# First maximum pass over four PSUM banks, page clears and a late load moved, side steps of a turn re-placed, gathers two groups sooner

## The reference, cut to what matters

```
h = layernorm(x) * (1 + ca) + sa
q, k, v = split(h @ qkv_w.T + qkv_b);  q, k = rope(q), rope(k)
attn = softmax(causal(q k^T / sqrt(8)));  x = x + ga * (attn v @ proj_w.T + proj_b)
h = layernorm(x) * (1 + cb) + sb
probs = sigmoid(h @ router_w.T + expert_bias); top 8 of 160, weights scaled by 2.5 / their sum
x = x + gb * (sum over the 8 experts of w_down(silu(w_gate h)) + shared expert)
```

## Time and profile before

| What | Value |
|---|---|
| median of 3 runs | 2018.66 us (2017.83 to 2021.72) |
| the profiled execution, its own time | 2040.86 us |
| its span, first to last instruction | 2038.9 us |
| mean granted TensorE clock | 0.887 |
| PE, DVE, ACT, POOL busy | 77%, 58%, 41%, 50% of the span |

### The profile page before, as it was taken

How to read it: one execution, slowest core, us unless ns; L and a number is a source line. 1 busy time by engine, 2 the same in 40 slices (tenths; PEclk the granted TensorE clock), 3 DMA queues, 4 the chain that set the end, 5 groups by cost and what they waited for, 6 DMA issues and landing times.

```text
span 2038.9 us, 35388 instructions
## 1 busy us (share of the span) xinstructions
PE 1565.4 (77%) x12102; PEld 792.8 (39%) x12102; DVE 1185.1 (58%) x2998; ACT 826.2 (41%) x1717; POOL 1021.8 (50%) x1057
## 2 busy tenths in 40 slices
PE   5558877788788778877877668966888888888875
PEld 2224433343343334333333345643444444444431
DVE  4657876687678767777766526633444444444434
ACT  1045544453445445445544434323343333343421
POOL 2001355555665556555645510056666666666663
PEclk9989888997898779778977678978999999999988
DMA  5695455554555545545542258986777777777631
GB/s 161 178 303 159 140 150 149 167 158 141 158 167 157 143 135 168 143 140 170 168 113 74 79 188 283 334 274 185 240 237 229 212 240 222 239 239 239 207 106 56
DMA packets 264986, 369.70 MB, mean 181 GB/s; under 512 B 41207, under 2 KB 141832, under 8 KB 264680
## 3 DMA queue, kind: packets, MB, share of 16 engines
q1 hardware_dynamic: 214248, 268.81, 45.5%
q0 software_dynamic: 28672, 58.78, 9.5%
q10 hardware_dynamic: 21888, 39.86, 5.2%
HBM read 219.69 MB, written 147.60 MB: 180 GB/s over the span
## 4 chain that ended last, share of the span: by engine, by line
PE 46%; DVE 20%; issue 12%; another core or an unknown queue 12%; ACT 5%; SPq 2%; DMA 2%; ACTq 1%; POOL 1%; DVEq 0%
DVE block_max L598 9%; PE bank L1715 6%; PE bank L743 5%; PE bank L1739 4%; PE bank L1578 4%; PE bank L1557 3%; PE bank L1594 3%; PE bank L569 3%; PE bank L680 2%; ACT prob L707 2%; PE bank L692 2%; PE bank L452 2%; PE bank L582 2%; PE bank L1720 1%
## 5 line engine op out<-in xcount | busy, mean ns | idle before, releaser
L1646 POOL DMA_INDIRECT vh<-results,pos_all x448 | 454.3, 1014 | 351.6 <-PE bank L1313 125.3
L818 POOL DMA_INDIRECT pages<-h,pos_s x448 | 433.2, 967 | 262.5 <-issue 103.7
L598 DVE TENSOR_REDUCE block_max<-bank 128x4 f32<-128x512 f32 x640 | 411.9, 683 | 245.7 <-PE bank L582 112.6
L707 ACT ACTIVATE prob<-bank 128x512 f32<-128x512 f32 x640 | 349.4, 598 | 465.9 <-PE bank L692 245.3
L1733 DVE TENSOR_TENSOR work<-work,bank 128x512 f32<-128x512 f32 x160 | 110.1, 688 | 358.1 <-issue 187.8
L569 PE MATMUL bank<-km,qm 64*128 64x512 bf16 (+3 forms) x1024 | 203.2, 343 | 112.2 <-DVE block_max L598 65.7
L680 PE MATMUL bank<-qe,ke 64*128 64x512 bf16 (+3 forms) x1024 | 174.9, 341 | 96.3 <-issue 57.2
L743 PE MATMUL bank<-prob,v_ext 128*32 128x512 f32 (+3 forms) x2048 | 225.7, 506 | 8.3 <-issue 5.3
L1608 ACT ACTIVATE v_ext<-bank 128x256 f32<-128x256 f32 x254 | 87.0, 387 | 199.9 <-remote 84.3
L569 PEld LDWEIGHTS bank<-km,qm 64*128 64x128 bf16 x1024 | 51.6, 97 | 276.6 <-issue 164.6
L1594 PE MATMUL bank<-prob,ke 64*128 64x128 f32 x1216 | 114.4, 309 | 52.3 <-ACT ke L1586 37.0
(11 more groups left out here) (221 smaller groups left out, 2542.4 us busy)
## 6 DMA issues: line engine op xcount, KB each, us to landing
prob<-wexp SPq DMA_DIRECT2D x448, 96.0 KB
pages<-free_rows SPq DMA_DIRECT2D x38, 1024.0 KB
prob<-pages SPq DMA_DIRECT2D x152, 256.0 KB
results<-v_ext ACTq DMA_DIRECT2D x152, 256.0 KB
qm<-q_stacks SPq DMA_DIRECT2D x64, 256.0 KB
km<-k_stacks SPq DMA_DIRECT2D x64, 256.0 KB
qe<-q_stacks SPq DMA_DIRECT2D x64, 256.0 KB
ke<-k_stacks SPq DMA_DIRECT2D x64, 256.0 KB
```

What stands on the lines that cost most here:

```text
L598: e.tensor_reduce(block_max[:, at, :], MX[g % 2][:, :].rearrange("p (k t) -> p k t", t=P), AX.X, ALU.max).then_inc(s_mxd, 1)
L707: e.activation(prob[:, slot, :], ST[g % 3][:, :], ACT.Exp, scale=SCALE).then_inc(s_exa, 1)
L818: e.indirect_dma_start(out=pages, in_=h2[:, t, :], in_offset=None, out_offset=bass.IndirectOffsetOnAxis(ap=pos_s[:, t * TOPK + k:t * TOPK ...
L1646: e.indirect_dma_start(out=y8[:, i, k, :], out_offset=None, in_=results[0:ready(n) * GRP * P, :], in_offset=bass.IndirectOffsetOnAxis(ap=p ...
```

## The change

- The first maximum pass (n = 0) uses banks 0 to 3 in turn, and a unit waits for the reduction of unit g - 4. The four projections of sequence 0 go to banks 6, 4, 5 and 3 and don't wait for DVE's reading of each other.
- The stores of q and k are split: four of the six transfers wait only for the second part (ACT, line 491), two for the third (POOL, line 495).
- Clears: of the twelve first ones, none are in turn -1, five in turn 0 and six in turn 1; the pairs come one turn later (turns 2 to 14). The load of sequences 9 to 15 moves from turn 0 to turn 2 with a semaphore of its own.
- Places: new lists for `pre` and for the two halves of the routing; the end of the maximum pass from 0.015 to 0.037 (ACT at 0.054, SP at 0.071), the first exponential load from 0.03 to 0.077, the two next maximum loads from 0.87 to 0.92 to 0.962; the page table's counts from 0.55 to 0.9 to 0.33 to 0.66 of turn 15.
- Last routing: spread over 0.9 of a merge with 34 groups instead of 0.62 of 30; both exponentials of ACT in one step; the reciprocal of line 1185 cut in four steps. The row numbers of the gathers are worked out at group 34 instead of 32.
- Gathers of tile T at group 49 + 2T instead of 51 + 2T, and its sum two groups sooner too.

```diff
-Q_RUNS = ((0, (0, 0, 0)), (3, (1, 1)), (5, (2,)))
-K_RUNS = ((0, (0, 1, 2)), (3, (0, 1)), (5, (0,)))
+Q_SOON, Q_LAST = ((0, (0, 0, 0)), (3, (1, 1))), ((5, (2,)),)
+K_SOON, K_LAST = ((3, (0, 1)), (5, (0,))), ((0, (0, 1, 2)),)
+        FIRST_MX = bank[0:4]
...
-                    e.wait_ge(s_x, (16, 32, 48, 80)[n])
+                    e.wait_ge(s_x, 16 * (n + 1))
+                if n == 9:
+                    e.wait_ge(s_x9, 16)
...
+                to_a, to_b = (MA, MA) if n > 0 else (MA, bank[4]) if w == "q" else (bank[5], bank[3])
-                    else:
+                    elif n > 0:
                         pre_d.wait(e, prev + "_b", n)
-                    pre_p.done(e.matmul(MA[:, :], col["w" + w], hT[:, :], start=True, stop=True), w + "_a")
+                    pre_p.done(e.matmul(to[:, :], col["w" + w], hT[:, :], start=True, stop=True), w + "_a")
...
+                    if runs in (Q_LAST, K_LAST):
+                        pre_g.wait(e, w + "_3", n)
+                    else:
+                        pre_a.wait(e, w + "_2", n)
...
-            steps = steps[:8] + stores[0:1] + steps[8:] + stores[1:2]
+            steps = steps[:8] + stores[0:2] + steps[8:] + stores[2:4]
...
+            banks = FIRST_MX if n == 0 else MX
+            mine = banks[g % len(banks)]
-                wait(e, s_mxd, n * 4 * UNITS + g - 1)
+                wait(e, s_mxd, n * 4 * UNITS + g + 1 - len(banks))
...
-            def sigmoid(e):
-                full_a.wait(e, "exp", m)
-                full_d.done(e.tensor_scalar(logit[:, :, :], logit[:, :, :], 1.0, 0.4, ALU.add, ALU.mult), "one")
-                full_d.wait(e, "one", m)
-                full_d.done(e.reciprocal(logit[:, :, :], logit[:, :, :]), "sig")
+            def sigmoid(e, t):
+                if t == 0:
+                    full_a.wait(e, "exp", m)
+                    full_d.done(e.tensor_scalar(logit[:, :, :], logit[:, :, :], 1.0, 0.4, ALU.add, ALU.mult), "one")
+                    full_d.wait(e, "one", m)
+                last = e.reciprocal(logit[:, t, :], logit[:, t, :])
+                if t == NT - 1:
+                    full_d.done(last, "sig")
...
-            steps.append({"dve": choose, "act": sig})
-            steps.append({"dve": weigh, "act": exps})
-            steps += [{"dve": f} for f in (sigmoid, combine_weights, part1, part2)]
+            steps.append({"dve": choose, "act": lambda e: [sig(e), exps(e)]})
+            steps.append({"dve": weigh})
+            steps += [{"dve": lambda e, t=t: sigmoid(e, t)} for t in range(NT)]
+            steps += [{"dve": f} for f in (combine_weights, part1, part2)]
...
-        PRE_AT = (0.021, 0.061, 0.15, 0.207, 0.274, 0.36, 0.422, 0.474, 0.481, 0.553, 0.611, 0.636, 0.688, 0.751)
+        PRE_AT = (0.003, 0.036, 0.154, 0.193, 0.273, 0.360, 0.438, 0.468, 0.470, 0.470, 0.563, 0.590, 0.590, 0.617, 0.633, 0.704)
...
-                streams.append((core(i), 0.0, 0.98, 0.95))
+                streams.append((core(i), 0.0, 0.978, 0.95))
-                streams.append(([{"pe": end_turn, "act": end_keep, "sp": end_store}], 0.015, 0.015))
-                streams.append((exp_loads(i, (0,)), 0.03, 0.03))
-                streams.append((exp_loads(i, (1,)), 0.28, 0.28))
-                streams.append((exp_loads(i, (2,)), 0.53, 0.53))
-                streams.append((exp_loads(i, (3,)), 0.78, 0.78))
-            if i <= 0:
-                streams.append((first_clears()[(0, 1, 5)[i + 2]:(1, 5, Z0)[i + 2]], (0.6, 0.45, 0.2)[i + 2], 0.9))
-                if i > -2:
-                    streams.append((x_loads(2, 4) if i == -1 else x_loads(4, 9) + x_loads(9, NB), 0.1, 0.6))
-            elif i < PAGED:
-                streams.append((clears(i), 0.3, 0.7))
+                streams.append(([{"pe": end_turn, "act": end_keep, "sp": end_store}], 0.037, 0.034))
+                streams.append((exp_loads(i, (0,)), 0.077, 0.077))
+                streams.append((exp_loads(i, (1,)), 0.276, 0.276))
+                streams.append((exp_loads(i, (2,)), 0.511, 0.511))
+                streams.append((exp_loads(i, (3,)), 0.798, 0.798))
+            if i <= 1:
+                streams.append((first_clears()[(0, 1, 1, 6)[i + 2]:(1, 1, 6, Z0)[i + 2]], (0.6, 0.45, 0.15, 0.15)[i + 2], 0.9))
+                if i in (-1, 0):
+                    streams.append((x_loads(2, 4) if i == -1 else x_loads(4, 9), 0.1, 0.6))
+            elif i <= PAGED:
+                streams.append((clears(i - 1), 0.3, 0.7))
+            if i == 2:
+                streams.append((x_loads(9, NB, s_x9), 0.15, 0.15))
...
-                streams.append((max_loads(i + 2, (0, 1)), 0.87, 0.92))
+                streams.append((max_loads(i + 2, (0, 1)), 0.962, 0.962))
...
-                streams.append((table(), 0.55, 0.9))
+                streams.append((table(), 0.33, 0.66))
...
-        FIRST, SPREAD = 30, 32
+        FIRST, SPREAD = 34, 32
...
-            return 51 + 2 * T
+            return 49 + 2 * T
...
-                        if k == SPREAD and name == "dve":
+                        if k == FIRST and name == "dve":
...
-            return merge((routing(NB - 1), 0.0, 0.62, 0.6), ([b_step(G) for G in range(FIRST)], 0.02, 1.0, 0.0))
+            return merge((routing(NB - 1), 0.0, 0.9, 0.6), ([b_step(G) for G in range(FIRST)], 0.02, 1.0, 0.0))
```

More of the change, by code:

```diff
@@ L231, in build @@
         MX, ST, PV, MA, MB = bank[0:2], bank[2:5], bank[5], bank[6], bank[7]
-        s_w, s_const, s_x, s_zero, s_set, s_zfill, s_rest = (
-            sem(n) for n in ("s_w", "s_const", "s_x", "s_zero", "s_set", "s_zfill", "s_rest"))
+        FIRST_MX = bank[0:4]
+        s_w, s_const, s_x, s_x9, s_zero, s_set, s_zfill, s_rest = (
+            sem(n) for n in ("s_w", "s_const", "s_x", "s_x9", "s_zero", "s_set", "s_zfill", "s_rest"))
         s_modd, s_modp, s_moda = sem("s_modd"), sem("s_modp"), sem("s_moda")
@@ L362, in mcol, with x_loads @@
             return mod[:, j, bass.ds(n, 1)]
-        def x_loads(first, last):
+        def x_loads(first, last, landed=s_x):
             return [{"sp": lambda e: e.dma_start(
                 xr[:, first * NT:last * NT, :].rearrange("p (n t) d -> p n t d", t=NT),
-                x[first:last].rearrange("n (t p) d -> p n t d", p=P)).then_inc(s_x, 16)}]
+                x[first:last].rearrange("n (t p) d -> p n t d", p=P)).then_inc(landed, 16)}]
         ZG = 4
@@ L457, in rope_a, with proj_b, rope_b @@
                         pre_d.wait(e, "q", n)
-                    pre_d.done(e.scalar_tensor_tensor(out=rot_a[:, :], in0=MA[:, :], scalar=col["b" + w], in1=cosT,
+                    pre_d.done(e.scalar_tensor_tensor(out=rot_a[:, :], in0=to[:, :], scalar=col["b" + w], in1=cosT,
                                                       op0=ALU.add, op1=ALU.mult), w + "_a")
-                def proj_b(e, w=w):
-                    pre_d.wait(e, w + "_a", n)
-                    pre_p.done(e.matmul(MA[:, :], col["w" + w + "r"], hT[:, :], start=True, stop=True), w + "_b")
-                def rope_b(e, w=w):
+                def proj_b(e, w=w, to=to_b):
+                    if n > 0:
+                        pre_d.wait(e, w + "_a", n)
+                    pre_p.done(e.matmul(to[:, :], col["w" + w + "r"], hT[:, :], start=True, stop=True), w + "_b")
+                def rope_b(e, w=w, to=to_b):
                     pre_p.wait(e, w + "_b", n)
-                    pre_d.done(e.scalar_tensor_tensor(out=rot_b[:, :], in0=MA[:, :], scalar=col["b" + w + "r"],
+                    pre_d.done(e.scalar_tensor_tensor(out=rot_b[:, :], in0=to[:, :], scalar=col["b" + w + "r"],
                                                       in1=sinT, op0=ALU.add, op1=ALU.mult), w + "_b")
@@ L496, in part3, with store @@
                                w + "_3")
-                def store(e, w=w):
-                    pre_g.wait(e, w + "_3", n)
+                def store(e, runs, w=w):
+                    if runs in (Q_LAST, K_LAST):
+                        pre_g.wait(e, w + "_3", n)
+                    else:
+                        pre_a.wait(e, w + "_2", n)
                     stacks = (qd if w == "q" else kd)[bass.ds(n, 1)].rearrange("o a r (g t) -> (o a) r g t", t=S)
-                    for first, parts in (Q_RUNS if w == "q" else K_RUNS):
+                    for first, parts in runs:
                         m = len(parts)
@@ L512, in pre @@
                 steps.append({"act": part2, "pool": part3})
-                stores.append({"sp": store})
+                soon, last = (Q_SOON, Q_LAST) if w == "q" else (K_SOON, K_LAST)
+                stores += [{"sp": lambda e, f=store, runs=runs: f(e, runs)} for runs in (soon, last)]
             def v_proj(e):
@@ L576, in hide @@
                 if m == 1:
-                    return e.matmul(MX[g % 2][:, at:at + 64], corner, eye_half[rows_, :],
+                    return e.matmul(mine[:, at:at + 64], corner, eye_half[rows_, :],
                                     start=False, stop=True, skip_group_check=True)
```

(6 more changed lines are left out.)

21 lines of the change are left out of this document (9 added, 12 removed).

## The result

The changed kernel takes 2030.97 us (median of 6 runs, 2024.6 to 2038.43), the kernel before 2020.35 on the same chip (6 runs): ratio 1.0057, interval [1.0032, 1.0082]. It is slower by 0.6%; the forecast was 2% faster. Its profiled execution took 2037.12 us (span 2035.2) against 2040.86. The profiled execution of the kernel before is 20 us over its median, that of the changed one 6 us, so the two spans hide the loss and I compare stretches.

The account below looks back on a forecast made before the run. No single engine was taken as the limit; PE was nearest, with step order deciding its lost time. Terms summed to 40.7 us off the profiled 2040.86, giving 2000.2, times 0.989: 1978 us, range 1955 to 2000.

Parts of the forecast that it names:

- the gathers' term: End of the kernel: last gathers wait for the last results whatever their number; one weighing comes off, 1.2 us won.
- Projections and first pass: Sequence 0's projections run back to back, 2.5 us off; four banks overlap PE and DVE in first maximum pass, 14 off.
- Turns 0 and 1: Moved clears and input load remove two thirds of PE's load waits, 13 us, less 4 in turn 1: net 9 off.
- my sign: Turn 0, expected if the forecast was right: no wait for a load over 4 us.
- rival 1: Turns 0 and 1: the clog only moves, 9 us given back, and the places gain nothing: 1996 us, chance 0.15.
- The end of each pass: End of each maximum pass: PE's wait at the turning of the maxima goes; 6 us off, ends 11 and 0.
- The other places: Side steps and loads at new places in the turns: a new order takes or gives a little; 3 us off.
- Tail: Routing of the last two sequences: cut reciprocal, no table load, chain spread over more groups; 5 us off, ends 8 and 0.
- Rival 2: First maximum pass is paced by its loads, 7 us won instead of 14: 1985 us, chance 0.12.
- rival 3: New places pay 1 us more in each of thirteen turns and PE's 11 us are all won: 1961 us, chance 0.16.
- rival 5: Whole change: the parts don't do what they say, or undo each other: 2018 us, chance 0.02.
- Rival 4: Slower: first exponential load, 3.2 us later in each of fourteen turns, comes after its quad is due: 2034 us, chance 0.05.

Follow-up runs that it names:

- a_burst: Changed kernel with gathers at 51 + 2T, the first 16 gathers of each sequence let go at once: 2097.66 us, 1.0364 of the kernel before.
- r_f50: Changed kernel with gathers at group 50 + 2T instead of 49 + 2T: 1980.58 us, 0.9767 of the kernel before.
- a_f51: Changed kernel with gathers back at group 51 + 2T, sums following: 1996.97 us, 0.9789 of the kernel before.
- u_clears: Changed kernel with gathers at 51 + 2T, clears and input loads put back at their old turns: 2011.96 us, 0.9858 of the kernel before.
- u_places: Changed kernel with gathers at 51 + 2T; old place lists, turning of the maxima, loads and table put back: 1999.96 us, 0.9792 of the kernel before.
- r_f49: The changed kernel as it is, gathers at 49 + 2T, run again on another chip: 2033.66 us, 1.0035 of the kernel before.
- r_f51: Changed kernel with gathers at 51 + 2T, on the same chip as r_f49: 1983.18 us, 0.9798 of the kernel before.
- a_run8: Changed kernel with gathers at 51 + 2T, first 8 of each sequence let go at once, on the faster chip: 1764.04 us, 0.9901 of the kernel before.
- a_f50: Changed kernel with gathers at 50 + 2T, on the faster chip: 1774.06 us, 0.9920 of the kernel before.
- r_run8: Changed kernel with gathers at 51 + 2T, first 8 of each sequence let go at once, on r_f49's chip: 1998.03 us, 0.9882 of the kernel before.
- set 4: Runs on one chip of a_run8 and a_f50 beside the kernel before, there 1783.65 us: ratios 0.9901 and 0.9920.

## Why the prediction was wrong

**The step that failed is the gathers' term**: "The last sequence's gathers wait for the last results ... whatever the number ..., and stay paced by the units", priced at 1.2 us won. I costed this part only at its end. It touches every sequence. The first gather of sequence n needs the results of group 47 + 8n; their store stands in the step of group 49 + 8n. At 51 + 8n it has landed, at 49 + 8n it is just being issued. I had asked of every other moved step what stands in front of it, but not of this one, though the earlier trace rows show a first gather let go by just such a landing. What it costs is not the wait itself (5 us of an engine that isn't the limit) but the run that follows: a_burst has the run without the wait and loses more, r_f50 has waits of up to 3 us, a run of over 9 gathers in only 2 of 12 sequences, and loses nothing. The cost is 2.4 to 2.7%, 48 to 55 us, instead of 1.2 us won. The run is long because POOL has little time to spare: four gathers a group at 1.26 us are 5.0 us of the 6.1 us that a group takes before (556 / 91), so by this estimate it makes up some 1 us a group. "Stay paced by the units" failed there. Why a run holds the other engines was found only as far as the last section says.

**The other steps.** Without the gathers my sum is 39.5 us, and a_f51 to before is 2.1% or 42 us. That agreement is partly luck, since the terms were off both ways:

- Projections and first pass: 16.5 forecast, 18 measured. The pass ends at 70.0 (forecast 72), and DVE's idle time is 5.2 us (forecast under 5): one load is 6.0 us late where I had left some 3 us, and the 3 us of other pauses aren't there. The mechanism held.
- Turns 0 and 1: 9 forecast, 14 measured by u_clears, the pass's own 2 us among them. Three waits of PE for loads, of 0.8, 4.5 and 4.4 us, are left of 19.2; the 4.5 stand in turn 0, where my sign was none over 4. The rule I weighed against this (the Trainium skill, DMA: Bandwidth & Descriptors, Issuing engines are not separate DMA queues) says that queues share the engines, and I took from it that a moved clear only moves its load. Here the load moved to where transfers had room; turn 1 at a share of 0.77 instead of 0.58 was no longer. The first half of rival 1, that the clog only moves, falls; its second half, that the places gain nothing, is what u_places measured.
- The end of each pass: 6 forecast. The wait left, as foretold, and nothing was won: in u_places it is back and the time is the same. PE's weight loads wait for the reductions instead. The lower end, 0, was the right value, by the reason that I gave and then discounted, that PE isn't the only limit. The other places: 3 forecast, nothing measured (1 us within 6 for both).
- Tail: 5 forecast, 16 measured. I priced the reciprocal's stall, which is the small part; the longer spread over 34 groups is the large one, and I had it under "other small pauses". That DVE's chain of routing steps stood between the groups, and that the spread lets PE's groups pass, is argued: the 173 us instead of 187 from group 0 to 60 agree with it.

**The rivals.** Rival 2 (the first pass paced by its loads) falls with the end at 70.0 us, rival 3 (the new places pay in every turn) with u_places, and rival 5 with the first pass. Rival 4, the slower case, named a late exponential load: turns 2 to 14 stayed as long as they were (68.6 us in the median of turns 2 to 13, as before), so it was the right sign by a wrong mechanism. The chance of 0.05 for slower was too small because I had looked for a slower case only in stage A, where most of the diff lies, and not at the one-line edits.

## What to carry to other kernels

When a consumer is moved ahead, look up the step that issues its producer's store and add the landing: here one group sooner cost nothing, and one more turned a paced stream into runs. An engine that isn't the limit can still stop the others if its work comes in one lump; pace its transfers. And undo a part before believing in it: a wait that leaves the list may have gone to the next line of it.

## What wasn't expected of the hardware

**Runs of indirect gathers hold the other engines.** Each gather holds POOL for 0.96 us and comes 0.30 us behind the last. By the Trainium skill (Perfetto Trace Analysis, DMA Instruction — SWDGE (GPSIMD)) that interval is the writing of descriptors, not the moving of data; no run here separates the two. In runs of 8 or 9 gathers of the kernels with paced gathers PE's longest pause within the run is mostly under 1.5 us (2.4 at most); in a_burst's of 15 to 20 it is 4.8 to 12.3 in all but one. The transfer engines are 41% and 49% busy in the two windows shown, and what the others wait for has been done, as far as the views show.

**What comes late is TensorE's semaphore update.** The traces also hold the semaphore events. The update of PE's last product of line 1609 in the a_burst timeline stands at 1521.28 us: 8.65 us behind the product's end, which the profile models, and 0.02 us ahead of ACT's start. Laid beside the ends of their instructions, the recorded updates of ACT, DVE and POOL follow by 0.01 us in every run that I took (before, a_f51, r_f49, r_f50, r_f51, a_burst, a_run8, a_f50). Those of PE come at most 0.24 us late until POOL's first indirect transfer in stage A, and on time again in stage B until the first gather; with the gathers they don't. Between groups 60 and 151 some 510 to 570 of PE's 682 updates are recorded, and 107 to 145 of them come over 2 us late. Over 5 us late are 1 to 6 in before, a_f51, r_f50 and r_f51, 18 in r_run8, 38 in r_f49, 46 in the changed kernel and 64 in a_burst; those of the last four all fall into runs of 10 or more gathers. So the products are done and the others learn of it late. The modelled ends can be trusted that far, since in a_run8 the same updates follow them by under 0.25 us. What holds the updates back isn't settled: I had no run that takes the gathers' transfers from their descriptors.

**One chip didn't show it.** In set 4 the kernel before took 1783.65 us, 12% less than elsewhere. In a_run8 most turns take 58 to 60 us instead of 67 to 69, and the 448 gathers stand in a single run from 1158 to 1754 us. Up to the third maximum pass it is no faster (179.6 us, a_f51 179.8); the turns are shorter from there, where POOL's indirect transfers begin (210 us). Windows of a_run8, groups 60 to 151:

```profile
1190.00:1678.00 488.00, 445.49 (x2514) 234.33 (x2516) 236.69 (x415) 224.39 (x499) 376.43 (x367) 0.97 0.84 264
```

Its longest waits:

```profile
ACT prob L719 <- PE bank L704: 260.5, 196, 8.3
ACT v_ext L1623 <- PE bank L1609: 185.1, 123, 13.9
...
DVE vh L1671 <- DMA vh<-results,pos_all: 153.9, 45, 7.9
```

No wait in it has an unnamed releaser, and no recorded update of PE in a_run8 or a_f50 comes more than 0.25 us late, gathers or not. a_f51 on the usual kind has many such waits, in stage A too:

```profile
DVE block_max L610 <- remote: 107.0, 26, 7.5
...
POOL vh L1661 <- remote: 81.5, 64, 2.5
ACT ke L1601 <- remote: 80.0, 34, 4.6
```

So the late updates come only where two things meet, POOL's indirect transfers and one of the other chips (or their state). That the 12% are the late updates, and that they are a trait of the chip, is argued from one chip, not shown. On that chip the gathers themselves pace stage B, DVE waits 154 us for their rows, and a_f50 gains only 0.8%. I have no run of f = 49 or 51 there, so whether the place matters on it stays open.
